# Softmax maxima of an attention kernel: subtracted over whole q tiles, or sent by DMA into a spare row of q

## The chip, the cores and the metric

The kernel is one program on one core of a Trainium2 chip. Its time is the device time of one execution in microseconds (us); several executions give a median. The core has a matrix engine (TensorE, in the profile PE, its weight loads PEld), a vector engine (VectorE, DVE), a scalar engine (ScalarE, ACT), GpSimd (POOL) and a sync engine (SyncE, SP), which here only issues transfers (DMAs).

## What is computed

The input `x` is (16, 512, 128) in float32. Six residual stages follow each other; the first three (a mixture of experts, a linear attention, the experts again) are the front part, which the change leaves alone, and the last three are the back part:

```
x = x + 0.5 * mlp(norm(x))          # front part ends with this one
x = x + attention(norm(x))          # back part, below
x = x + 0.5 * mlp(norm(x))          # back part: w1 (128 x 512), relu, w2

def attention(x):                   # 16 heads of 8 columns, 512 positions
    xn = layernorm(x) * scale + bias
    q, k, v = heads(xn @ wq), heads(xn @ wk), heads(xn @ wv)
    probs = softmax(q @ k.T / sqrt(128))
    return merge(probs @ v) + xn
```

The softmax subtracts the maximum of each row of scores before the exponential, and divides by the row's sum after the product with v.

## The kernel before

The back part (`build_back`) takes one of 16 batches of 512 positions after the other. Heads go in four groups g of four; in a group each head j has a strip of 32 partitions. `qt[g]` and `kt_[g]` hold q and k of a group with the head's 8 numbers as high and low parts in rows 0 to 23 of a strip. Row 24 (`MAX_ROW`) of k's strips is one, and of q's strips zero. These tiles are made by way of memory: `stage` writes the parts (`khi`, `klo`, `qhi`, `qlo`) to a staging buffer, `fetch` reads two 256 KB tiles per group back.

Scores are computed twice. `first_scores` (L1379) makes rows of scores for a block of 128 queries into a bank `MX`, and DVE's `maximum` (L1263) reduces it to the maximum of each query, in tile `nm`. Once the 16 maxima columns of a group are there, PE transposes `nm` (small work "nm": four 128x128 transposes, L1341) and DVE subtracts the result from the q tile into `qm` (L1220). The second scores (L1366, into a bank `ST`) use `qm`: row 24 is then minus the maximum, times k's one. ACT takes the exponential (L1163), and `weighted` (L1394, eight recorded matmuls a step, into `PV`) multiplies by v.

A batch is 16 steps k, written out by hand and the same on every engine. In step k PE issues: `ST` and `MX` matmuls of heads 0 and 1, then `weighted` of step k-1, then those of heads 2 and 3, then the step's small work. The `MX` matmuls and the maxima run `AHEAD` steps before the `ST` matmuls. The table `SMALL` says which small work stands at the end of which step, as (name, batch relative to this one, number):

- xt, kp, qp, v: transposed input, then k, q and v of the next batch. ACT copies the high part of xt, kp, qp; DVE subtracts it (`xl`, `klo`, `qlo`) after the second maximum of the following step.
- nm: the transpose of the maxima. ot: the outputs of a head group transposed, then divided by DVE (L1230, L1232).
- ft, g, y: input, four hidden blocks and two output halves of the MLP of the previous batch; `fl` is ft's low part on DVE.

Results go to seven PSUM banks in two rings. v and g use the three `ST` banks, all other small work the four `MX` banks, in the order in which PE issues them (`ST_RING`, `MX_RING`); `wait_bank` makes a matmul wait until the entry four places (three in `ST`) before it in the ring has been read. DVE also does two layer-norm statistics (`stats`), for the next batch at the start of step 0 and for the MLP input at the start of step 3; GpSimd turns them into `xn`, `xf` and `zf`.

SP issues all transfers in one queue, in program order, and waits in between for the semaphores that free or fill a tile.

Of the kernel before, what the change touches and what calls it, by code (L numbers as in the profile page):

```python
# [106 lines left out]
def build_front(nc, weights, x_dram, mid_dram, ident_dram, turns):  # L107
# [739 lines left out]

AHEAD = 6  # L850
# [30 lines left out]
def build_back(nc, weights, mid_dram, out_dram, staged_dram, tail_dram, batches):  # L881
    w = weights
    with ExitStack() as ctx:
# [16 lines left out]
        khi, klo, qhi, qlo = (sb(n, [P, T, P], F32R) for n in ("khi", "klo", "qhi", "qlo"))  # L900
        qt = [sb(f"qt{g}", [P, T, P], F32R) for g in range(GRP)]
        kt_ = [sb(f"kt{g}", [P, T, P], F32R) for g in range(GRP)]
        qm = [sb(f"qm{k}", [P, T, P], F32R) for k in range(2)]
        nm = [sb(f"nm{k}", [P, T, P]) for k in range(2)]
        va = [sb(f"va{p}", [P, T, H, 32]) for p in range(2)]
        pr = [sb(f"pr{k}", [P, HG, N]) for k in range(2)]
        oTs = [sb(f"oTs{k}", [P, T, P]) for k in range(2)]
# [93 lines left out]
        @block.sync  # L1001
        def _(sp):
            def stage(B, which, tile, part):

                sp.dma_start(staged_dram[B.parity, which][:, part * DH:(part + 1) * DH, :],
                             tile[:].rearrange("p a b -> p (a b)").bitcast(F32)).then_inc(staged.sem, 16)

            def stage_batch(B):
                if not B.exists:
                    return  # L1010
                sp.wait_ge(khi_ready.sem, B.at(khi_ready, 1))
                stage(B, 0, khi, 0)
                free_strips(B, 0)
                stage(B, 0, khi, 1)
                sp.wait_ge(used["kp"].sem, B.at(used["kp"], 1))
                stage(B, 0, klo, 2)
                sp.wait_ge(qhi_ready.sem, B.at(qhi_ready, 1))
                stage(B, 1, qhi, 0)
                stage(B, 1, qhi, 2)
                sp.wait_ge(used["qp"].sem, B.at(used["qp"], 1))  # L1020
                stage(B, 1, qlo, 1)
                if B.first:
                    sp.wait_ge(preset, 64)
                sp.wait_ge(staged.sem, B.at(staged, 16 * 6))

            def free_strips(B, g):

                if not B.first:
                    sp.wait_ge(made["st"].sem, B.at(made["st"], HG * T * (g + 1) - UNITS))

            def fetch(B, g):

                if not B.exists:
                    return
                if g > 0:
                    free_strips(B, g)
                for which, tile in ((0, kt_[g]), (1, qt[g])):
                    sp.dma_start(tile[:].rearrange("p a b -> p (a b)").bitcast(F32),
                                 staged_dram[B.parity, which][g * HG:(g + 1) * HG].rearrange("h r n -> (h r) n")
                                 ).then_inc(fetched[g].sem, 16)  # L1040

            def batch_steps(B):
                nxt, prv, ahead = B + 1, B + -1, B + 2
                if ahead.exists:
                    if B.exists:

                        sp.wait_ge(xx_ready.sem, B.at(xx_ready, 1))
                    p = ahead.parity
                    sp.dma_start(x[p][:], md[ahead.number + PAD]).then_inc(loaded[p].sem, 16)
                fetch(B, 3)  # L1050
                stage_batch(nxt)
                for g in range(3):
                    fetch(nxt, g)
                if prv.exists:
                    p = prv.parity
                    sp.wait_ge(used["y"].sem, prv.at(used["y"], 2))
                    sp.dma_start(od[prv.number], res[p][:]).then_inc(stored[p].sem, 16)

            sp.dma_start(x[0][:], md[PAD]).then_inc(loaded[0].sem, 16)
            for p in range(2):  # L1060
# [124 lines left out]
        def _(dve):  # L1185
# [14 lines left out]
            def small(B, rel, name, n):  # L1200
# [14 lines left out]
                elif name == "ft":  # L1215
                    dve.wait_ge(fh_ready.sem, C.at(fh_ready, 1))
                    nc.vector.tensor_tensor(fl[:], m[:], fh[:], ALU.subtract).then_inc(used["ft"].sem, 1)
                elif name == "nm":
                    dve.wait_ge(made["nm"].sem, C.at(made["nm"], n + 1))
                    nc.vector.tensor_tensor(qm[n % 2][:], qt[n][:], m[:], ALU.subtract).then_inc(used["nm"].sem, 1)  # L1220
                elif name == "ot":
                    dve.wait_ge(made["ot"].sem, C.at(made["ot"], n + 1))
                    if n > 0 or not C.first:
# [30 lines left out]
            def maximum(B, rel, u):  # L1254

                C = B + rel
                if not C.exists:
                    return
                g, t, j = u // (HG * T), u // HG % T, first_head(u)
                dve.wait_ge(made["mx"].sem, C.at(made["mx"], u + 1))  # L1260
                c = 32 * j + MAX_ROW
                bank = MX[MX_PLACE["mx", rel, u] % MX_BANKS]
                nc.vector.tensor_reduce(nm[g % 2][:, t, c:c + 1], bank[:].rearrange("p a b -> p (a b)"), AX.X,  # L1263
                                        ALU.max).then_inc(used["mx"].sem, 1)

            def batch_steps(B):
                for k in range(STEPS):
# [7 lines left out]
                    maximum(B, rel, s * HG + 2)  # L1275
                    maximum(B, rel, s * HG + 3)
                    for name, r, n in SMALL[k]:
                        if name not in FOR_ACT + BY_BOTH:
                            small(B, r, name, n)

            for k in range(2):
# [5 lines left out]
        def _(pe):  # L1287
# [22 lines left out]
            def small(B, rel, name, n):  # L1310
# [26 lines left out]
                                       skip_group_check=True)  # L1337
                elif name == "nm":
                    pe.wait_ge(used["mx"].sem, C.at(used["mx"], (n + 1) * HG * T))
                    for t in range(T):  # L1340
                        mm = pe.transpose(m[:, t], nm[n % 2][:, t], w["ident"][:])  # L1341
                elif name == "ot":
                    pe.wait_ge(pv_out.sem, C.at(pv_out, n + 1))
                    for t in range(T):
# [12 lines left out]
            def scores(B, k, j):  # L1357
# [2 lines left out]
                    return  # L1360
                g, u = k // T, k * HG + j
                if k % T == 0 and j == 0:
                    pe.wait_ge(used["nm"].sem, B.at(used["nm"], g + 1))
                place = ST_PLACE["st", 0, u]
                wait_bank(B, ST_RING, ST_BANKS, place)
                pe.matmul(flat(ST[place % ST_BANKS]), kt_[g][rows_of(j), k % T], flat(qm[g % 2])[rows_of(j)], start=True,  # L1366
                          stop=True).then_inc(made["st"].sem, 1)

            def first_scores(B, rel, u):
# [297 lines left out]
```

## Time and profile before

| | |
|---|---|
| median of 3 executions | 2253.99 us (2253.25 to 2261.86) |
| profiled execution, its own time | 2249.78 us |
| its span, first to last instruction | 2248.0 us |
| PE busy | 1996.7 us (89%) |
| DVE busy | 1687.3 us (75%) |
| ACT busy | 1083.7 us (48%) |
| GpSimd busy | 585.0 us (26%) |
| granted clock of PE, mean | 0.970 |
| transfers | 85.28 MB, mean 38 GB/s |

The back part fills the span from about 1295 us on. A share of the span says little here, as the front part has other limits; the rows are read in the back part alone, and one batch of it in the window 1700 to 1760 us. Busy times of single instructions overlap: two maxima of 0.68 us that follow each other start 0.60 us apart. In a timeline, a row "x4" holds four instructions that ran on without a gap worth telling; its time is from the first's start to the last's end.

### The profile page before, as it was taken

How to read it: one execution, taken by the hardware profiler on the slowest of the kernel's cores; microseconds unless marked ns; L12 is line 12 of the kernel's file. 1: busy time of each engine (PE TensorE's matmuls, PEld its weight loads, DVE VectorE, ACT ScalarE, POOL GpSimd, SP SyncE). 2: the span in 40 equal slices, each digit the busy share in tenths (PEclk: the TensorE clock that was granted, in tenths of full speed). 3: DMA queues.
4: the chain of work that ended last, by engine and by line, in shares of the span. 5: the costliest groups of instructions: out<-in, count | busy, mean ns of one | idle time of the engine just before them, and what ended most of it. 6: DMA issues, size and time to landing. Idle time of an engine off the chain costs nothing. (4 is left out here: it accounts for less than half of the span.)

```text
span 2248.0 us, 34225 instructions
## 1 busy us (share of the span) xinstructions
PE 1996.7 (89%) x12660; PEld 1369.6 (61%) x12660; DVE 1687.3 (75%) x4160; ACT 1083.7 (48%) x1907; POOL 585.0 (26%) x621
## 2 busy tenths in 40 slices
PE   3998989898999899889989758999999999999997
PEld 3787778777877787777877623444444444444443
DVE  5767776767766776767677449888888888888882
ACT  3333323333333333333333117777777777777774
POOL 2331332223222323233313031222222222222211
PEclk9999999999999999999999959999999999999999
DMA  3000000000000000000000032222222222222220
GB/s 117 6 10 10 1 10 10 10 1 10 10 10 5 6 10 10 10 1 10 10 6 1 10 98 71 76 76 76 76 75 76 76 76 76 76 76 79 70 69 10
DMA packets 47941, 85.28 MB, mean 38 GB/s; under 512 B 5728, under 2 KB 9056, under 8 KB 47712
## 3 DMA queue, kind: packets, MB, share of 16 engines
q1 hardware_dynamic: 45872, 81.32, 11.4%
q8 instruction: 101, 1.65, 0.3%
q10 hardware_dynamic: 1904, 1.78, 0.2%
q14 instruction: 64, 0.52, 0.1%
HBM read 49.26 MB, written 34.87 MB: 37 GB/s over the span
## 5 line engine op out<-in xcount | busy, mean ns | idle before, releaser
L1263 DVE TENSOR_REDUCE b_nm<-b_MX 128x1 f32<-128x512 f32 x1024 | 647.6, 682 | 74.1 <-PE b_MX L1379 66.8
L1163 ACT ACTIVATE b_pr<-b_ST 128x512 f32<-128x512 f32 x1024 | 550.8, 601 | 163.1 <-PE b_ST L1366 161.9
L1379 PE MATMUL b_MX<-b_kt,b_qt 32*128 32x512 f32 x1024 | 353.9, 511 | 43.0 <-DMA b_qt<-staging 10.1
L383 ACT ACTIVATE s<-G 128x512 f32<-128x512 f32 x306 | 182.9, 598 | 432.7 <-PE G L685 423.7
L690 PE MATMUL Y<-w_wd,h 128*128 128x128 f32 x2448 | 335.3, 281 | 8.6 <-DVE h L544 7.9
L690 PEld LDWEIGHTS Y<-w_wd,h 128*128 128x128 f32 x2448 | 315.4, 195 | 24.0 <-DVE h L544 13.3
L535 DVE TENSOR_TENSOR su<-U,s 128x512 f32<-128x512 f32 x272 | 186.1, 684 | 161.3 <-ACT s L383 83.3
L1366 PEld LDWEIGHTS b_ST<-b_qm,b_kt 32*128 32x128 f32 x1024 | 119.1, 185 | 304.6 <-ACT b_pr L1163 190.8
L1366 PE MATMUL b_ST<-b_qm,b_kt 32*128 32x512 f32 x1024 | 293.6, 503 | 10.8 <-ACT b_pr L1163 10.7
L1394 PE MATMUL b_PV<-b_pr,b_va 128*32 128x512 f32 x2048 | 280.5, 620 | 0.0
L544 DVE TENSOR_TENSOR h<-C,su 128x512 f32<-128x512 f32 x272 | 188.1, 691 | 9.3
L1379 PEld LDWEIGHTS b_MX<-b_kt,b_qt 32*128 32x128 f32 x1024 | 140.0, 187 | 79.7 <-DVE b_nm L1263 15.5
L683 PE MATMUL U<-xh,w_wuh 128*128 128x512 f32 x306 | 128.2, 419 | 57.5 <-DVE su L535 44.0
L305 POOL TENSOR_TENSOR vpe_s<-mv_s,w_eps 128x4 f32<-128x4 f32 x33 | 6.6, 199 | 627.3 <-DVE mv_s L437 627.3
L1082 POOL TENSOR_TENSOR b_ve<-b_mv,w_eps_two 128x4 f32<-128x4 f32 x16 | 3.2, 201 | 617.5 <-DVE b_mv L1197 617.4
L683 PE MATMUL G<-xh,w_wgh 128*128 128x512 f32 x306 | 145.7, 476 | 0.0
L685 PE MATMUL G<-xl,w_wgh 128*128 128x512 f32 x306 | 121.2, 396 | 0.0
L685 PE MATMUL U<-xl,w_wuh 128*128 128x512 f32 x306 | 121.1, 396 | 0.0
L684 PE MATMUL G<-xh,w_wgl 128*128 128x512 f32 x306 | 121.0, 395 | 0.0
L684 PE MATMUL U<-xh,w_wul 128*128 128x512 f32 x306 | 120.8, 395 | 0.0
L683 PEld LDWEIGHTS U<-xh,w_wuh 128*128 128x128 f32 x306 | 57.7, 189 | 96.9 <-DVE su L535 58.8
L718 PE MATMUL C<-cT,w_pairs 128*128 128x512 f32 x272 | 109.6, 403 | 0.0
(237 smaller groups left out, 3497.3 us busy)
## 6 DMA issues: line engine op xcount, KB each, us to landing
b_kt<-staging SPq DMA_DIRECT2D x64, 256.0 KB, 2.9
b_qt<-staging SPq DMA_DIRECT2D x64, 256.0 KB, 3.4
staging<-b_khi SPq DMA_DIRECT2D x32, 256.0 KB, 3.0
staging<-b_qhi SPq DMA_DIRECT2D x32, 256.0 KB, 3.0
xin<-in_x SPq DMA_DIRECT2D x17, 256.0 KB, 2.6
mid<-xo SPq DMA_DIRECT2D x17, 256.0 KB, 2.0
b_x<-mid SPq DMA_DIRECT2D x16, 256.0 KB, 2.9
staging<-b_klo SPq DMA_DIRECT2D x16, 256.0 KB, 3.0
```

The costliest lines, as they stand in the source:

```text
L383: nc.scalar.activation(sbuf_s[n % 2][:], G[n % 2][:], ACT.Silu).then_inc(act_done.sem, 1)
L535: nc.vector.tensor_tensor(out[:], U[:], sbuf_s[n % 2][:], ALU.mult).then_inc(up_used.sem, 1)
L544: nc.vector.tensor_tensor(h[n % 3][:], C[:], su[n % 2][:], ALU.mult).then_inc(h_ready.sem, 1)
L683: pe.matmul(flat(bank), wh, flat(high), start=True, stop=False)
L684: pe.matmul(flat(bank), wl, flat(high), start=False, stop=False)
L685: return pe.matmul(flat(bank), wh, flat(low), start=False, stop=True)
L690: mm = pe.matmul(bank[:, t], hid[:, t], wd, start=(first and t == 0), stop=True, skip_group_check=True)
L1163: nc.scalar.activation(pr[k % 2][:, j], bank[:].rearrange("p a b -> p (a b)"), ACT.Exp, scale=SM_SCALE).then_inc(used["st"].sem, 1)
L1263: nc.vector.tensor_reduce(nm[g % 2][:, t, c:c + 1], bank[:].rearrange("p a b -> p (a b)"), AX.X, ALU.max).then_inc(used["mx"].sem, 1)
L1366: pe.matmul(flat(ST[place % ST_BANKS]), kt_[g][rows_of(j), k % T], flat(qm[g % 2])[rows_of(j)], start=True, stop=True).then_inc(made["st"] ...
L1379: pe.matmul(flat(MX[place % MX_BANKS]), qt[g][rows_of(j), u // HG % T], flat(kt_[g])[rows_of(j)], start=True, stop=True).then_inc(made["mx ...
L1394: mm = pe.matmul(flat(PV)[rows_of(j)], va[B.parity][:, kt, g * HG + j], pr[k % 2][:, j], start=(kt == 0), stop=(kt == T - 1), skip_group_c ...
```

## The change

The subtraction over q tiles goes, and `qm` with it: the second scores read `qt[g]` itself. The maxima of a group are kept as 16 columns of a 128x32 tile. PE transposes it in one matmul into 32 rows of a bank, ACT copies these with factor -1 into `nr`, and SP sends them in four transfers of 4 rows of 128 numbers (2 KB each) into row 24 of the four strips of `qt[g]` (`shift`). PE waits for these transfers (`shift_in[g]`) before the first `ST` matmul of a group. `AHEAD` is 7 where it was 6, and `SMALL` is rearranged.

```diff
-AHEAD = 6
+AHEAD = 7
 SMALL = [
-    [], [("ot", -1, 3)], [("nm", 0, 1)], [("xt", 1, 0)],
-    [("kp", 1, 0)], [("ot", 0, 0), ("qp", 1, 0)], [("nm", 0, 2)], [("ft", -1, 0)],
-    [("g", -1, 0)], [("ot", 0, 1), ("g", -1, 1)], [("nm", 0, 3)], [("g", -1, 2)],
-    [("g", -1, 3)], [("ot", 0, 2)], [("nm", 1, 0), ("y", -1, 0)], [("v", 1, 0), ("y", -1, 1)]]
+    [], [("nm", 0, 1), ("ot", -1, 3)], [("xt", 1, 0)], [("kp", 1, 0)],
+    [("qp", 1, 0)], [("nm", 0, 2), ("ot", 0, 0)], [("v", 1, 0)], [("ft", -1, 0)],
+    [("g", -1, 0)], [("nm", 0, 3), ("ot", 0, 1)], [("g", -1, 1)], [("g", -1, 2)],
+    [("g", -1, 3)], [("nm", 1, 0), ("ot", 0, 2)], [("y", -1, 0)], [("y", -1, 1)]]
...
-        qm = [sb(f"qm{k}", [P, T, P], F32R) for k in range(2)]
-        nm = [sb(f"nm{k}", [P, T, P]) for k in range(2)]
+        nm = [sb(f"nm{k}", [P, 32]) for k in range(2)]
+        nr = [sb(f"nr{k}", [32, P], F32R) for k in range(2)]
...
+            def shift(C, g):
+                if not C.exists:
+                    return
+                sp.wait_ge(used["nm"].sem, C.at(used["nm"], g + 1))
+                for t in range(T):
+                    sp.dma_start(qt[g][MAX_ROW::32, t].bitcast(F32),
+                                 nr[g % 2][t * HG:(t + 1) * HG].bitcast(F32)).then_inc(shift_in[g].sem, 16)
...
+                elif name == "nm":
+                    if n >= 2 or not C.first:
+                        before = (C, n - 2) if n >= 2 else (C + -1, n + GRP - 2)
+                        act.wait_ge(shift_in[before[1]].sem, before[0].at(shift_in[before[1]], 16 * T))
+                    nc.scalar.activation(nr[n % 2][:], m[0:32, 0], ACT.Copy, scale=-1.0).then_inc(used["nm"].sem, 1)
...
-                elif name == "nm":
-                    nc.vector.tensor_tensor(qm[n % 2][:], qt[n][:], m[:], ALU.subtract).then_inc(used["nm"].sem, 1)
...
-                    for t in range(T):
-                        mm = pe.transpose(m[:, t], nm[n % 2][:, t], w["ident"][:])
+                    mm = pe.transpose(m[0:32, 0], nm[n % 2][:], w["ident"][:])
...
-                    pe.wait_ge(used["nm"].sem, B.at(used["nm"], g + 1))
+                    pe.wait_ge(shift_in[g].sem, B.at(shift_in[g], 16 * T))
```

On PE, between the steps 9 and 10 of a batch, stood the transposes of a group's outputs and the three matmuls of a hidden block, then the matmuls of step 10 (before):

```order
L1345 MATMUL b_MX<-w_ident,b_oTs 128x128 x4
L1292 MATMUL b_ST<-b_fh,w_w1h 128x512
L1293 MATMUL b_ST<-b_fh,w_w1l 128x512
L1294 MATMUL b_ST<-b_fl,w_w1h 128x512
L1366 MATMUL b_ST<-b_qm,b_kt 128x512
L1379 MATMUL b_MX<-b_kt,b_qt 128x512
L1366 MATMUL b_ST<-b_qm,b_kt 128x512
L1379 MATMUL b_MX<-b_kt,b_qt 128x512
L1394 MATMUL b_PV<-b_pr,b_va 32x512 x4
```

In the same place of the changed kernel the one transpose of the maxima and those of the outputs stand, and the hidden block comes a step later:

```order
L1362 MATMUL b_MX<-w_ident,b_nm 32x128
L1366 MATMUL b_MX<-w_ident,b_oTs 128x128 x4
L1387 MATMUL b_ST<-b_qt,b_kt 128x512
L1400 MATMUL b_MX<-b_kt,b_qt 128x512
L1387 MATMUL b_ST<-b_qt,b_kt 128x512
L1400 MATMUL b_MX<-b_kt,b_qt 128x512
L1415 MATMUL b_PV<-b_pr,b_va 32x512 x4
```

Two entries of the `MX` ring now stand between the last `MX` matmul of step 9 and the first of step 10, where one stood; the same holds after the steps 1, 5 and 13.

On PE at the turn from one batch to the next stood, before, the last of v's twelve matmuls and the MLP's second output half:

```order
L1335 MATMUL b_ST<-w_wvl,b_xh 128x128
L1336 MATMUL b_ST<-w_wvh,b_xl 128x128
L1350 MATMUL b_MX<-w_w,b_hid 128x128 x8
L1366 MATMUL b_ST<-b_qm,b_kt 128x512
L1379 MATMUL b_MX<-b_kt,b_qt 128x512
```

In the changed kernel:

```order
L1400 MATMUL b_MX<-b_kt,b_qt 128x512
L1371 MATMUL b_MX<-w_w,b_hid 128x128 x8
L1387 MATMUL b_ST<-b_qt,b_kt 128x512
L1400 MATMUL b_MX<-b_kt,b_qt 128x512
```

The twelve matmuls for v moved to the end of step 6.

On DVE, from the maxima of the steps 0 and 1 to the low part of q (before):

```order
L1263 TENSOR_REDUCE b_nm<-b_MX 128x1 x4
L1220 TENSOR_TENSOR b_qm<-b_qt,b_MX 128x512
L1191 BN_STATS b_stf<-b_xf 128x6 x4
L1195 MEMSET b_nudge 128x1
L1197 BN_AGGR b_mvf<-b_stf 128x2 x4
L1263 TENSOR_REDUCE b_nm<-b_MX 128x1 x6
L1208 TENSOR_TENSOR b_xl<-b_MX,b_xh 128x512
L1263 TENSOR_REDUCE b_nm<-b_MX 128x1 x4
L1211 TENSOR_TENSOR b_klo<-b_MX,b_khi 128x512
```

In the changed kernel:

```order
L1285 TENSOR_REDUCE b_nm<-b_MX 128x1 x4
L1213 BN_STATS b_stf<-b_xf 128x6 x4
L1217 MEMSET b_nudge 128x1
L1219 BN_AGGR b_mvf<-b_stf 128x2 x4
L1285 TENSOR_REDUCE b_nm<-b_MX 128x1 x2
L1230 TENSOR_TENSOR b_xl<-b_MX,b_xh 128x512
L1285 TENSOR_REDUCE b_nm<-b_MX 128x1 x4
L1233 TENSOR_TENSOR b_klo<-b_MX,b_khi 128x512
L1285 TENSOR_REDUCE b_nm<-b_MX 128x1 x4
L1236 TENSOR_TENSOR b_qlo<-b_MX,b_qhi 128x512
```

The subtraction `qm` is gone, and the low parts come one step (four maxima) earlier, while the statistics stay where they were.

## Rows read from the trace of the kernel before

**Rows 1.** The page: busy time of each engine (share of the span), number of instructions.

```profile
PE 1996.7 (89%) x12660; PEld 1369.6 (61%) x12660; DVE 1687.3 (75%) x4160; ACT 1083.7 (48%) x1907; POOL 585.0 (26%) x621
```

**Rows 2.** Chain that ended last, window 1700 to 1760 us, shares by line.

```profile
by line: DVE b_nm L1263 23.8%; PE b_PV L1394 17.7%; PE b_ST L1366 16.9%; PE b_MX L1350 6.1%; PE b_MX L1379 4.9%; PE b_MX L1345 3.9%; PE b_ST L1292 3.6%; PE b_ST L1293 2.3%; PE b_ST L1294 2.3%; DVE b_qm L1220 2.0%; PE b_MX L1341 2.0%; issue 
```

**Rows 3.** Groups by line, 1340 to 2248 us: busy us, mean ns | idle before.

```profile
L1263 DVE TENSOR_REDUCE b_nm<-b_MX 128x1 f32<-128x512 f32 x997 | 631.2, 682 | 63.7 <-PE b_MX L1379 56.4
...
L1220 DVE TENSOR_TENSOR b_qm<-b_qt,b_MX 128x512 fp32r<-128x512 f32 x63 | 42.6, 676 | 1.9 <-PE b_MX L1341 1.9
```

**Rows 4.** Timeline of PE, 1700 to 1760 us: start us, us, what.

```profile
1701.36 1.07 PE L1394 MATMUL b_PV<-b_pr,b_va 128*32 128x512 f32 x8
...
1704.53 1.06 PE L1394 MATMUL b_PV<-b_pr,b_va 128*32 128x512 f32 x8
...
1705.96 0.66 PE L1341 MATMUL b_MX<-w_ident,b_nm 128*128 128x128 f32 x4
...
1707.26 1.06 PE L1394 MATMUL b_PV<-b_pr,b_va 128*32 128x512 f32 x8
...
1713.54 1.07 PE L1394 MATMUL b_PV<-b_pr,b_va 128*32 128x512 f32 x8
...
1716.28 1.06 PE L1394 MATMUL b_PV<-b_pr,b_va 128*32 128x512 f32 x8
...
1720.55 1.07 PE L1394 MATMUL b_PV<-b_pr,b_va 128*32 128x512 f32 x8
...
1721.98 0.33 PE L1334 MATMUL b_ST<-w_wvh,b_xh 128*128 128x128 f32 x1
...
1723.37 2.00 PE L1350 MATMUL b_MX<-w_w,b_hid 128*128 128x128 f32 x16
...
1726.31 1.07 PE L1394 MATMUL b_PV<-b_pr,b_va 128*32 128x512 f32 x8
...
1750.31 1.06 PE L1394 MATMUL b_PV<-b_pr,b_va 128*32 128x512 f32 x8
...
1753.04 1.07 PE L1394 MATMUL b_PV<-b_pr,b_va 128*32 128x512 f32 x8
...
1756.76 1.07 PE L1394 MATMUL b_PV<-b_pr,b_va 128*32 128x512 f32 x8
```

**Rows 5.** Timeline of DVE, the same window.

```profile
1704.66 2.72 DVE L1263 TENSOR_REDUCE b_nm<-b_MX 128x1 f32<-128x512 f32 x4
1707.30 0.68 DVE L1220 TENSOR_TENSOR b_qm<-b_qt,b_MX 128x512 fp32r<-128x512 f32 x1
...
1731.85 0.25 DVE L1230 RECIPROCAL b_rden<-b_MX 128x16 f32<-128x16 f32 x1
...
1732.34 2.47 DVE L1263 TENSOR_REDUCE b_nm<-b_MX 128x1 f32<-128x512 f32 x4
...
1740.08 0.68 DVE L1208 TENSOR_TENSOR b_xl<-b_MX,b_xh 128x512 fp32r<-128x512 f32 x1
...
1743.91 0.68 DVE L1211 TENSOR_TENSOR b_klo<-b_MX,b_khi 128x512 fp32r<-128x512 f32 x1
...
1748.12 0.68 DVE L1214 TENSOR_TENSOR b_qlo<-b_MX,b_qhi 128x512 fp32r<-128x512 f32 x1
...
1754.27 0.68 DVE L1217 TENSOR_TENSOR b_fl<-b_MX,b_fh 128x512 fp32r<-128x512 f32 x1
```

**Rows 6.** Timeline of GpSimd, the same window: the last operation of `xn`.

```profile
1732.35 1.28 POOL L1098 TENSOR_TENSOR b_xn<-b_xn,w_lnsb 128x512 f32<-128x512 f32 x1
```

**Rows 7.** Timeline of SP's queue: one transfer issued behind another.

```profile
1752.46 0.43 SPq L1038 DMA_DIRECT2D b_qt<-staging  x1
```

**Rows 8.** Transfers by line: count, KB each, median us from issue to landing.

```profile
b_qt<-staging SPq DMA_DIRECT2D x64, 256.0 KB, 3.4
...
w_bq<-in_bq SPq DMA_DIRECT2D x1, 0.5 KB, 6.4
```

**Rows 9.** Groups of ACT, whole span: the smallest reads of a PSUM bank.

```profile
L362 ACT ACTIVATE lb<-Z 128x64 f32<-128x64 f32 x34 | 7.6, 223 | 66.5 <-PE Z L677 66.5
```

More of the change, by code:

```diff
@@ L856 @@
 SMALL = [
[4 rows of a table removed]
[4 rows of a table added]
 FOR_ACT = ("v", "g")
 BY_BOTH = ("xt", "kp", "qp", "ft")
+IN_ACT = FOR_ACT + BY_BOTH + ("nm",)
 def ahead_of(k):
@@ L939, in build_back @@
         fetched = [sig(f"fetched{g}", 32) for g in range(GRP)]
+        shift_in = [sig(f"shift_in{g}", 16 * T) for g in range(GRP)]
         preset = ctx.enter_context(nc.semaphore("b_preset"))
@@ L1023, in stage_batch @@
                     sp.wait_ge(preset, 64)
-                sp.wait_ge(staged.sem, B.at(staged, 16 * 6))
             def free_strips(B, g):
@@ L1050, in batch_steps @@
                 fetch(B, 3)
+                shift(B, 1)
                 stage_batch(nxt)
-                for g in range(3):
-                    fetch(nxt, g)
+                shift(B, 2)
+                if nxt.exists:
+                    sp.wait_ge(staged.sem, nxt.at(staged, 16 * 6))
+                fetch(nxt, 0)
+                fetch(nxt, 1)
+                shift(B, 3)
+                fetch(nxt, 2)
+                shift(nxt, 0)
                 if prv.exists:
@@ L1130, in small @@
                 C = B + rel
-                if not C.exists or name not in FOR_ACT + BY_BOTH:
+                if not C.exists or name not in IN_ACT:
                     return
@@ L1217, in small @@
                     nc.vector.tensor_tensor(fl[:], m[:], fh[:], ALU.subtract).then_inc(used["ft"].sem, 1)
-                elif name == "nm":
-                    dve.wait_ge(made["nm"].sem, C.at(made["nm"], n + 1))
-                    nc.vector.tensor_tensor(qm[n % 2][:], qt[n][:], m[:], ALU.subtract).then_inc(used["nm"].sem, 1)
                 elif name == "ot":
@@ L1260, in maximum @@
                 dve.wait_ge(made["mx"].sem, C.at(made["mx"], u + 1))
-                c = 32 * j + MAX_ROW
+                if u % (HG * T) == 0 and (g >= 2 or not C.first):
+                    before = (C, g - 1) if g >= 2 else (C + -1, g + GRP - 1)
+                    dve.wait_ge(made["nm"].sem, before[0].at(made["nm"], before[1]))
+                c = t * HG + j
                 bank = MX[MX_PLACE["mx", rel, u] % MX_BANKS]
-                nc.vector.tensor_reduce(nm[g % 2][:, t, c:c + 1], bank[:].rearrange("p a b -> p (a b)"), AX.X,
+                nc.vector.tensor_reduce(nm[g % 2][:, c:c + 1], bank[:].rearrange("p a b -> p (a b)"), AX.X,
                                         ALU.max).then_inc(used["mx"].sem, 1)
@@ L1277, in batch_steps @@
                     for name, r, n in SMALL[k]:
-                        if name not in FOR_ACT + BY_BOTH:
+                        if name not in IN_ACT:
                             small(B, r, name, n)
@@ L1362, in scores @@
                 if k % T == 0 and j == 0:
-                    pe.wait_ge(used["nm"].sem, B.at(used["nm"], g + 1))
+                    pe.wait_ge(shift_in[g].sem, B.at(shift_in[g], 16 * T))
                 place = ST_PLACE["st", 0, u]
                 wait_bank(B, ST_RING, ST_BANKS, place)
-                pe.matmul(flat(ST[place % ST_BANKS]), kt_[g][rows_of(j), k % T], flat(qm[g % 2])[rows_of(j)], start=True,
+                pe.matmul(flat(ST[place % ST_BANKS]), kt_[g][rows_of(j), k % T], flat(qt[g])[rows_of(j)], start=True,
                           stop=True).then_inc(made["st"].sem, 1)
```

## The prediction

> **What bounds the kernel now.** I began with the busy times of the page. They leave no engine clearly ahead: PE 89% and DVE 75% of a span of which the back part, where the change is, is only the last two fifths [rows 1]. In the back part alone DVE is busy with maxima for most of the time, and still waits 56.4 us in all for the matmuls that feed them [rows 3]. So I read the chain of waits over one batch: it changes engines, about a quarter in the maxima and most of the rest in PE's matmuls, and the two things that the change attacks, the subtraction `qm` and the transposes of the maxima, hold 2.0% each of 60 us, 1.2 us each [rows 2]. A share of a chain is not a saving, because what comes late after it may be late anyway. Therefore I used the timelines of PE and DVE and cut a batch by the starts of the eight matmuls on `PV`, one set per step.
>
> Step 9 starts its set at 1701.36, step 0 of the next batch at 1726.31, step 9 again at 1756.76 [rows 4]. A batch is 24.95 + 30.45 = 55.4 us. The two parts have different limits. From step 9 to step 0 PE paces: a step with four transposes or none takes 2.73 (1704.53 to 1707.26), the two with a hidden block 6.28 together, the one with the maxima's transposes and the first output half 4.27, the one with v and the second half 5.76 [rows 4]. From step 0 to step 9 DVE paces, with maxima 0.60 apart and the low parts between them [rows 5].
>
> **Second half of a batch, steps 9 to 0.** The removed `qm` is worth nothing here, since DVE waits for PE. What counts is PE's own list. The transposes of the maxima leave the output step: 0.59 of 4.27 (1705.96 to the following matmul, just under the row's 0.66), 3.68 stays. v leaves the last step: its matmuls start 1.39 ahead of the output half [rows 4]; I take 1.45, so 4.31 stays of 5.76. That is 2.04 saved. Three hidden blocks in three steps cost 3 x 3.14 = 9.42, as two cost 6.28.
>
> The price stands in steps 9 and 13. Two entries of the `MX` ring follow each other there, so the second `MX` matmul of the next step reuses the bank of the fourth maximum of this step; with one entry it was the third's. In step 10 the maxima start 0.13 after the `PV` set (1704.66 against 1704.53) and the fourth is done at 2.77 (`qm` starts at 1707.30) [rows 4, 5]. Only then may that matmul start, and `PV` 0.43 later: 2.8 + 0.43 = 3.25 for such a step instead of 2.73. New sum: 3.25 + 9.42 + 3.25 + 3.68 + 4.31 = 23.91, against 24.95: 1.04 us less.
>
> **First half, steps 0 to 9.** I walk DVE from the start of step 2's maxima, 1732.34 [rows 5]. After step 1 there are two entries again. The last maximum of step 1 ends about 1731.9 (the reciprocal starts at 1731.85), so `PV` of step 2 starts at 1732.4, the third `MX` matmul 1.0 later and its maximum 0.5 after that, at 1733.87: DVE does two maxima, waits 0.3, does two, and reaches the statistics at 1735.08. From 1734.74 (four maxima) to `xl` at 1740.08 it now takes 5.34 for `qm`, statistics and six maxima [rows 5]. Without `qm` (0.59) and four maxima (2.40) 2.35 stays, so `xl` starts at 1737.43. Each low part holds a bank that the fourth `MX` matmul of its step needs, with a product behind it: `xl` to `klo` is 3.83 (1740.08 to 1743.91), and `klo` to `qlo` becomes the same: `qlo` at 1745.1. It was 1748.12, one step later.
>
> From `qlo` to the next `PV` set was 2.19 (1748.12 to 1750.31) with four transposes; with five, and the wait on the fourth maximum, I take 2.4: step 6 at 1747.5. Then comes v, in a step that PE paces: 4.27 - 0.59 - 1.85 (an output half, a bit under the row's 2.00) + 1.45 = 3.3, where the plain step is 2.73. Step 8 starts at 1747.5 + 3.3 + 2.73 = 1753.5, and with `fl` and a hidden block 3.72 (1753.04 to 1756.76), plus 0.1 since its maxima can't start before their step, step 9 at 1757.35 [rows 4]. That is 31.04 from step 0 against 30.45: 0.59 us more. The early projections and the missing `qm` are eaten by v and by DVE's waits.
>
> **Work that lies beside.** The copy with factor -1 on ACT: not shown before. Between 0.22 (64 columns by 128 partitions) [rows 9] and 0.60 for a whole bank; for 128 columns I take 0.28, near the lower end. It comes after the fourth exponential, and the next one can't start before about 0.5 later, since the longer small work holds up its scores: hidden at 0.28, 0.1 out in the open at 0.60. GpSimd's `xn` is ready at 1733.63 [rows 6]; PE now wants it at 1732.4 + 1.43 = 1733.85. Hidden, with only 0.2 to spare.
>
> The four transfers: SP issues one per 0.43 [rows 7]. Tightest is group 3: copy done 3.3 after the `PV` set of step 9, last issue at 4.75, and PE wants the row at 3.25 + 6.28 - 0.43 = 9.1. So 4.3 us may pass until landing. Nothing so small between on-chip tiles is in the trace: the bounds are 3.4 for a fetch of 256 KB and 6.4 for 0.5 KB in a crowd of loads at the start [rows 8]. I take 3.4 or less, as the fetches stand in the same queue and the same part; hidden. The fetches that now queue behind a shift have a step or more to spare.
>
> SP goes on after 0.43 us, without waiting for the 3.4 us to landing [rows 7, 8], so transfers of one queue are under way together. The Trainium skill (DMA: Bandwidth & Descriptors, Rules for kernel authors) advises to merge small transfers, under 64 KB being mostly overhead, and its section Anatomy of one DMA has some 2 us fixed per transfer. Taken as four in a row that estimate would be 8 us, over the slack; overlapped, 2 us, and nothing. No row here shows a small one alone.
>
> **Sum.** Per full batch -1.04 + 0.59 = -0.45; 14 such batches: -6.3. The first batch has no MLP work to gain from and pays the two waits (+1.0); ahead of it v no longer stands before the first scores, against a seventh step of maxima (-0.7); the last batch -0.5. Together -6.5. The profiled execution took 2249.78 and would take 2243.3; the median is 4.2 above it, so I forecast **2247.5 us**. A measurement tells 0.5%, 11.3 us, from no change; this is less. By itself the forecast has 2238 to 2257, 0.7 us per batch to either side.
>
> **Rivals.**
> - *The work removed is all gained* (0.28). The 2.4 us of chain per batch [rows 2], less 0.4 for the remaining transpose, times 15 is 30 us: 2224. For it: the chain runs through both. Against it: the bank waits above. Without these waits alone (0.52 + 0.52 + 0.3) I would come to 2229.
> - *The shifted rows come late* (0.07), slower. If landing takes over 4.3 us, PE stands still at the first scores of a group. With 6.4 [rows 8] group 3 is 2.1 late, group 2 about 1.8, the others 0.5 together: 4.4 x 16 = 70 us, 2318. Against it: 3.4 for much more data. Should the four even land one after the other, 3.4 each, the last lands at 3.3 + 13.6 = 16.9, 7.8 late: 125 us for group 3 alone, 2372 or more (0.01 of the 0.07). [...]
> - *ACT's copy is in the way* (0.13), slower. ACT works in order; where it isn't hidden, 0.28 to 0.60 four times a batch is 18 to 38 us: 2265 to 2285, and PE idles before the scores on the exponentials. It decides once the copy waits for a transpose that DVE delays.
> - *v and the wait for `xn`* (0.06): if `xn` is 0.5 late, and the chain of k and q with it, 7 us are added: 2255.
>
> The forecast itself has 0.46. Faster by over 0.5%: all of the first rival and a sixth of the forecast, 0.36. Slower: the two middle rivals but for a part of the second of them, 0.17. The same: 0.47. The range of 8 in 10 is 2222 to 2268.
>
> **What would show it.** Right: `qm` gone from the chain; `PV` sets 3.2 to 3.3 apart after steps 1, 9 and 13, with PE waiting on the maxima there; last step of a batch 4.3; 55.0 us per batch; ACT's copy under 0.3; no wait of PE on a transfer to `qt`. Wrong: `PV` sets 2.8 apart after 9 and 13 (then the first rival), a PE wait on `qt` from `nr`, or step 6 far from 3.3.

## The result, and the profile after

| | median us (runs) | lowest to highest | profiled execution: us, span, clock |
|---|---|---|---|
| before | 2253.62 (6) | 2248.83 to 2264.79 | 2249.78, 2248.0, 0.970 |
| after | 2276.46 (6) | 2262.22 to 2282.18 | 2262.22, 2260.4, 0.964 |

After over before is 1.0084 [1.0056, 1.0112]: slower, by 23 us between the medians. The forecast was 2247.5 us, range 2222 to 2268: a little faster, and the kernel is slower, above the range. In a later comparison (10 runs of after, 25 of before) the ratio was 1.0059 [1.004, 1.0078], 17 us between the medians: the direction stands, and the size is known to some 6 us.

The six times of after line up with the mean granted clock of each run: 2262.2 and 2264.7 us at 0.964, 2275.7 at 0.957, 2277.2 to 2278.9 at 0.953 to 0.954, 2282.2 at 0.951. That was the first lead.

The page of after, answering to [rows 1], and below it the two groups of lines that answer to [rows 3], here over the whole span. Columns: busy us, mean ns | idle before, what ended most of it.

```profile
PE 2002.6 (89%) x12468; PEld 1356.4 (60%) x12468; DVE 1658.4 (73%) x4096; ACT 1089.2 (48%) x1971; POOL 584.8 (26%) x621
...
L1285 DVE TENSOR_REDUCE b_nm<-b_MX 128x1 f32<-128x512 f32 x1024 | 655.4, 683 | 123.6 <-PE b_MX L1400 114.7
...
L1400 PE MATMUL b_MX<-b_kt,b_qt 32*128 32x512 f32 x1024 | 363.2, 516 | 62.0 <-DVE b_xl L1230 23.0
```

DVE lost 64 instructions and 29 us of work, PE lost 192 matmuls, and yet PE is busy 6 us longer. The copy and the transfers behave as forecast: the copy of the maxima's row on ACT takes 256 ns, and SP issues four transfers in 2.27 us (the first row: groups of ACT from 1340 us on; the second: timeline of SP: start, us).

```profile
L1169 ACT ACTIVATE b_nr<-b_MX 32x128 fp32r<-32x128 f32 x63 | 16.1, 256 | 2.5 <-PE b_MX L1362 2.5
```

```profile
1756.38 2.27 SPq L1049 DMA_DIRECT2D b_qt<-b_nr  x4
```

Cut by the starts of the `PV` sets as in the prediction, a batch reads (us per step, steps 0 to 15; one batch of each kernel without a disturbance):

| | 0 | 1 | 2 | 3 | 4 | 5 | 6 | 7 | 8 | 9 | 10 | 11 | 12 | 13 | 14 | 15 | sum |
|---|---|---|---|---|---|---|---|---|---|---|---|---|---|---|---|---|---|
| before | 2.76 | 2.74 | 2.87 | 4.16 | 3.72 | 4.22 | 3.52 | 2.73 | 3.72 | 3.15 | 2.73 | 3.09 | 3.19 | 2.74 | 4.27 | 5.76 | 55.4 |
| after | 2.76 | 3.33 | 2.73 | 4.90 | 3.82 | 3.77 | 3.36 | 2.73 | 3.72 | 3.33 | 3.09 | 3.09 | 3.19 | 3.33 | 3.85 | 4.42 | 55.4 |

Undisturbed, the two kernels are equal. But 9 of the 14 full batches of after are longer than that, by 0.5 to 2.0 us, 10.9 us in all, in steps 3 to 5; step 3 goes up to 6.15, step 4 to 5.09, step 5 to 4.24. I call these disturbed. In before it is 5 of 14, 5.5 us in all, in steps 4 and 5, step 4 up to 5.00. In before they are batches 2, 5, 8, 11 and 14, every third one, so they are not scattered by chance. One of the long batches of after, timeline of PE (start, us, what, then in brackets idle before and what ended it):

```profile
1743.83 0.50 PE L1387 MATMUL b_ST<-b_qt,b_kt 32*128 32x512 f32 x1
1745.97 0.50 PE L1400 MATMUL b_MX<-b_kt,b_qt 32*128 32x512 f32 x1 [1.64 <-DVE b_xl L1230]
1746.40 0.50 PE L1314 MATMUL b_MX<-b_xh,w_wkh 128*128 128x512 f32 x1
...
1747.87 1.94 PE L1415 MATMUL b_PV<-b_pr,b_va 128*32 128x512 f32 x8
...
1750.65 0.79 PE L1314 MATMUL b_MX<-b_xh,w_wq1h 128*128 128x512 f32 x1
...
1752.96 1.72 PE L1415 MATMUL b_PV<-b_pr,b_va 128*32 128x512 f32 x8
...
1754.61 0.49 PE L1400 MATMUL b_MX<-b_kt,b_qt 32*128 32x512 f32 x1
```

The same `PV` set that takes 1.07 elsewhere takes 1.94 here, and a matmul of 0.50 takes 0.79. The windows of one microsecond name the reason (columns: length; busy us of PE, PEld, DVE, ACT, POOL with counts; PEclk; DMA share; GB/s):

```profile
1743.00:1744.00 1.00, 1.00 (x11) 0.17 (x3) 0.96 (x8) 1.00 (x3) 0.97 (x1) 1.00 0.00 0
1744.00:1745.00 1.00, 0.33 (x3) 0.01 (x3) 1.00 (x5) 0.82 (x3) 0.69 (x2) 1.00 0.00 0
1745.00:1746.00 1.00, 0.03 (x1) 0.03 (x1) 1.00 (x3) 0.45 (x1) 0.92 (x2) 1.00 0.00 0
...
1747.00:1748.00 1.00, 1.00 (x10) 0.33 (x12) 0.20 (x2) 0.60 (x2) 1.00 (x2) 0.75 0.00 0
1748.00:1749.00 1.00, 1.00 (x8) 0.06 (x6) 1.00 (x2) 1.00 (x2) 1.00 (x1) 0.50 0.00 0
...
1753.00:1754.00 1.00, 1.00 (x12) 0.16 (x8) 0.91 (x2) 0.94 (x2) 0.00 (x0) 0.50 0.00 0
1754.00:1755.00 1.00, 1.00 (x11) 0.19 (x3) 0.98 (x2) 0.14 (x1) 0.00 (x0) 0.83 0.79 182
```

PE is almost idle from 1744.3 to 1746.0, and from about 1747.5 to 1754.3 the granted clock is 0.50, that is 1.2 instead of 2.4 GHz. How did so long a wait come about? From the list of PE's waits in the back part of after (us in all, times, longest):

```profile
PE b_MX L1400 <- DVE b_xl L1230: 23.0, 14, 1.6
```

and of before:

```profile
PE b_MX L1326 <- DVE b_nm L1263: 14.6, 14, 1.0
...
PE b_MX L1379 <- DVE b_xl L1208: 4.7, 10, 0.5
```

Before, PE stood still 1.0 us ahead of the transposes of `xn` and 0.5 us for `xl`, with 3.1 us of matmuls between (timeline of PE in the same batch, before):

```profile
1737.23 0.66 PE L1326 MATMUL b_MX<-w_ident,b_xn 128*128 128x128 f32 x4 [1.04 <-DVE b_nm L1263]
...
1740.82 0.49 PE L1379 MATMUL b_MX<-b_kt,b_qt 32*128 32x512 f32 x1 [0.47 <-DVE b_xl L1208]
```

After, the transposes stand one step earlier, in step 2, ahead of the statistics of `xf` that DVE works off at the start of step 3. Maxima, statistics and `xl` then follow each other on DVE with nothing that PE could do between them, and its two waits are one, of 1.64 us. The timeline of DVE in the long batch above shows the row of work at whose end PE goes on (`xl` ends at 1745.92, the matmul starts at 1745.97):

```profile
1742.87 0.86 DVE L1213 BATCH_NORM_STATS2 b_stf<-b_xf 128x6 f32<-128x128 f32 x4
...
1744.07 1.26 DVE L1285 TENSOR_REDUCE b_nm<-b_MX 128x1 f32<-128x512 f32 x2
1745.24 0.68 DVE L1230 TENSOR_TENSOR b_xl<-b_MX,b_xh 128x512 fp32r<-128x512 f32 x1
```

The 12.4 us between the profiled executions divide so: up to the first `PV` set +1.3 (1340.85 to 1342.19), batch 0 +3.9, batches 1 to 14 +5.9 (of it 5.4 disturbances), batch 15 -0.1, the tail +1.3. The first of these differs as much between two executions of one kernel: in a second profile of after the first `PV` set starts at 1343.64. Batch 0 ran at a mean granted clock of 0.83 where it had 0.91 before, and the tail at 0.72 instead of 0.80; in the second profile of after batch 0 had 0.92 and was 0.8 us longer than before, so most of the 3.9 is the clock again. The tail was 26.4 us in both profiles of after, against 25.1.

### The profile page after: what moved, and what is told of

Same layout as the page of the kernel before. It is cut to its first block and busy times, and to the rows that moved or that the text cites. A ratio compares the mean times of both kernels' runs of the same rounds, so it can differ in the third digit from the quotient of the medians.

```text
span 2260.4 us, 34221 instructions
## 1 busy us (share of the span) xinstructions
PE 2002.6 (89%) x12468; PEld 1356.4 (60%) x12468; DVE 1658.4 (73%) x4096; ACT 1089.2 (48%) x1971; POOL 584.8 (26%) x621
## 5 line engine op out<-in xcount | busy, mean ns | idle before, releaser
L1285 DVE TENSOR_REDUCE b_nm<-b_MX 128x1 f32<-128x512 f32 x1024 | 655.4, 683 | 123.6 <-PE b_MX L1400 114.7
L1400 PE MATMUL b_MX<-b_kt,b_qt 32*128 32x512 f32 x1024 | 363.2, 516 | 62.0 <-DVE b_xl L1230 23.0
L1387 PE MATMUL b_ST<-b_qt,b_kt 32*128 32x512 f32 x1024 | 303.1, 507 | 11.1 <-ACT b_pr L1185 9.5
L1387 PEld LDWEIGHTS b_ST<-b_qt,b_kt 32*128 32x128 f32 x1024 | 122.6, 186 | 310.9 <-ACT b_pr L1185 201.4
L1415 PE MATMUL b_PV<-b_pr,b_va 128*32 128x512 f32 x2048 | 285.8, 632 | 0.0
L683 PE MATMUL U<-xh,w_wuh 128*128 128x512 f32 x306 | 127.9, 418 | 57.2 <-DVE su L535 44.1
```

The source lines that it names most:

```text
L683: pe.matmul(flat(bank), wh, flat(high), start=True, stop=False)
L1285: nc.vector.tensor_reduce(nm[g % 2][:, c:c + 1], bank[:].rearrange("p a b -> p (a b)"), AX.X, ALU.max).then_inc(used["mx"].sem, 1)
L1400: pe.matmul(flat(MX[place % MX_BANKS]), qt[g][rows_of(j), u // HG % T], flat(kt_[g])[rows_of(j)], start=True, stop=True).then_inc(made["mx ...
L1415: mm = pe.matmul(flat(PV)[rows_of(j)], va[B.parity][:, kt, g * HG + j], pr[k % 2][:, j], start=(kt == 0), stop=(kt == T - 1), skip_group_c ...
```

## The experiments

**Theory.** The path through the row costs nothing in a batch that runs undisturbed. The new order puts PE's waits together into one of 1.6 us, and around the end of this wait the clock falls in most batches. **Rivals:** the copy and the transfers cost the time; or the small slowings of single steps add up and the clock merely shows it.

### The order alone, and the path alone

The maxima by subtraction on DVE as before, with the order of after (7 steps ahead):

```
-AHEAD = 6
+AHEAD = 7
...
-    [], [("ot", -1, 3)], [("nm", 0, 1)], [("xt", 1, 0)],
-    [("kp", 1, 0)], [("ot", 0, 0), ("qp", 1, 0)], [("nm", 0, 2)], [("ft", -1, 0)],
-    [("g", -1, 0)], [("ot", 0, 1), ("g", -1, 1)], [("nm", 0, 3)], [("g", -1, 2)],
-    [("g", -1, 3)], [("ot", 0, 2)], [("nm", 1, 0), ("y", -1, 0)], [("v", 1, 0), ("y", -1, 1)]]
+    [], [("nm", 0, 1), ("ot", -1, 3)], [("xt", 1, 0)], [("kp", 1, 0)],
+    [("qp", 1, 0)], [("nm", 0, 2), ("ot", 0, 0)], [("v", 1, 0)], [("ft", -1, 0)],
+    [("g", -1, 0)], [("nm", 0, 3), ("ot", 0, 1)], [("g", -1, 1)], [("g", -1, 2)],
+    [("g", -1, 3)], [("nm", 1, 0), ("ot", 0, 2)], [("y", -1, 0)], [("y", -1, 1)]]
```

> The new step table and 7 steps ahead, with the old subtraction on DVE. Clock theory (the slower time of the changed kernel comes from one long wait of PE, 1.6 us on xl in step 3, after which the granted clock falls to 1.2 GHz for some microseconds in most batches): the wait stands here too and is longer by the subtraction after step 1 (0.6 us on DVE ahead of it), so step 3 is near 5 us or more, most batches lose 0.5 to 2 us to the clock, 2265 to 2290 us. Rival (the transfers, or ACT's copy, cost the time): without them it comes out at or below the kernel before, 2240 to 2255.

The row path with the order of before; the list of small work goes the other way round:

```
-AHEAD = 7
+AHEAD = 6
...
```

> The old step table and 6 steps ahead, with the new path of the maxima (one transpose, copy on ACT, four transfers). Clock theory: step 3 has two short waits as before, so as few disturbed batches as before (5 of 14); but only one full step lies between the maxima and the scores, so PE waits for the transfers in groups 1 to 3 if they land later than 2 us after the last issue: an undisturbed batch of 54 to 57 us, and the size of the waits measures the landing. Rival (the path itself is what costs): a batch over 56 us with waits that the changed kernel shows too.

| | median us (runs) | to before [95%] | undisturbed batch | disturbed of 14 |
|---|---|---|---|---|
| order alone | 2280.85 (4) | 1.0116 [1.0093, 1.0139] | 55.7 | 11 |
| path alone | 2276.48 (4) | 1.0106 [1.0076, 1.0136] | 56.4 | 1 |

Each half alone is slower than before, for different reasons. The order alone has the 1.6 us wait and the disturbed batches, up to 2.8 us longer each. (The expectation had the wait longer by the subtraction; it is the same, and step 3 takes 4.90.) PE's waits with the order alone:

```profile
PE b_MX L1379 <- DVE b_xl L1208: 23.6, 15, 1.6
```

The path alone has nearly no disturbed batch, 1 where 5 were expected, and without the subtraction its steps 3 and 6 are 0.4 us shorter each. But step 7 takes 3.75 instead of 2.73 and step 11 3.72 instead of 3.09, a batch 1.0 us more. Its first waits of PE in the back part are for the shifted row, which after does not wait for once (the 2.4 stands in the last batch, the longest in a full batch is 1.24, in step 7):

```profile
PE b_ST L1387 <- DMA b_qt<-b_nr: 42.8, 47, 2.4
PE b_ST L1387 <- ACT b_pr L1185: 9.7, 20, 1.1
PE b_MX L1348 <- DVE b_nm L1285: 8.9, 14, 0.7
```

The wait of 1.24 us stands in step 7 of all 14 full batches, and the clock falls behind one of them only (batch 11, steps 8 and 9 at 4.99 each). So a wait that stands alone and is shorter by 0.4 us did it once in 14, with batches of another length.

This run gives the price of landing, which before did not show. SP issues the four from 1745.65 on, and the score that needs the last of them starts at 1748.91 (timelines of SP and of PE with the path alone):

```profile
1745.65 2.15 SPq L1049 DMA_DIRECT2D b_qt<-b_nr  x4
```

```profile
1748.91 0.49 PE L1387 MATMUL b_ST<-b_qt,b_kt 32*128 32x512 f32 x1 [0.35 <-DMA b_qt<-b_nr]
```

The fourth is issued about 1747.3, half a microsecond ahead of the end of the row, so it was there at the latest 1.6 us after its issue (an estimate from these two rows). With 7 steps ahead this is hidden, with 6 not. So the new order hides the transfers that the path needs, and brings the wait with it.

### The same kernel with the wait filled

Six repetitions of one score matmul, in step 3, where PE waits for `xl`. They overwrite a score with itself and take 1.65 us; nothing else is changed.

```
+for extra in range(6 if (k, j) == (3, 3) else 0):
+    pe.matmul(flat(ST[place % ST_BANKS]), kt_[g][rows_of(j), k % T], flat(qt[g])[rows_of(j)],
+              start=True, stop=True)
```

> The changed kernel, in which PE issues the fourth score matmul of step 3 seven times instead of once (same operands, same bank), so that it has work for about 1.3 of the 1.6 us for which it waits for xl. Clock theory: the clock stays up, no more than 5 of 14 batches are disturbed, the undisturbed batch stays at 55.4 us, and the time falls by 8 to 15 us against the changed kernel, to 2250 to 2262. Rival (the clock falls for another reason, or its fall is not what costs): the same count of disturbed batches and 2265 to 2285 us.

Measured: 2260.51 us (10 runs), 1.0029 [1.0011, 1.0046] to before; 5 disturbed batches of 14 instead of 9. The undisturbed batch stays at 55.44: the extra work is free where PE stood. Timeline of PE in such a batch:

```profile
1804.70 1.65 PE L1388 MATMUL b_ST<-b_qt,b_kt 32*128 32x512 f32 x6
1806.19 0.39 PE L1390 MATMUL b_ST<-b_qt,b_kt 32*128 32x512 f32 x1
1806.84 0.50 PE L1403 MATMUL b_MX<-b_kt,b_qt 32*128 32x512 f32 x1 [0.25 <-DVE b_xl L1230]
```

Copy, transfers and undisturbed steps are those of after, so neither rival can make this difference. The count is still that of before, and not none. To have the comparison on one chip the changed kernel ran again, beside a version with more filling (8 repetitions in step 3, 3 each in steps 4 and 5):

> The changed kernel once more, beside the others on one chip. Clock theory: 2262 to 2282 us, and the executions line up by their mean granted clock (0.964 to 0.951), since only the count of disturbed batches differs; undisturbed batches stay at 55.4 us. Rival: the spread has another source and the clock is the same in slow and fast executions.

> As the filled kernel, with eight repeated score matmuls in step 3 and three each in steps 4 and 5, where PE waits 0.6 us for klo and qlo. Clock theory: fewer disturbed batches than with six (6 of 14), 2245 to 2260 us, the undisturbed batch at 55.4 to 55.7. Rival (repeating matmuls merely shifts other work): no fewer disturbed batches, and a longer undisturbed one.

After again: 2269.35 us (10), 1.0059 [1.004, 1.0078], 8 disturbed batches. More filling: 2261.3 (10), 1.0037 [1.0016, 1.0059], 4 disturbed batches of +1.15 each. More work for PE, and 8 us less between the medians; the two intervals overlap, so this pair alone would be a hint. It missed the 2245 to 2260 expected by a little (and the expectation counts 6 disturbed batches of the filled kernel, where it has 5): the filling of steps 4 and 5 brings nothing measurable, and the remaining drops come without a long wait in step 3.

### The statistics of xf moved away

`if k == 3 and prv.exists` decides where the statistics stand. In step 6 DVE has time for them:

```
-                if k == 3 and prv.exists:
+                if k == 6 and prv.exists:
```

> The changed kernel with the MLP's layer-norm statistics (1.2 us of DVE) at the start of step 6, where v's matmuls let DVE wait, instead of step 3. Clock theory: the wait for xl falls from 1.6 to about 0.4 us, few batches are disturbed, step 3 takes 3.7 to 3.9 us instead of 4.9 and step 6 stays near 3.4 to 3.6: 54.3 to 54.7 us per batch, 2225 to 2245 us in all. Rival (GpSimd's zf comes too late for step 7): PE waits there up to 1 us, and the batch stays over 55 us.

Measured: 2239.1 us (4), 0.9934 [0.9908, 0.996]. No batch of 14 is disturbed, and each takes 54.3: step 3 went from 4.90 to 3.72, which makes 16 us over 14 batches. That is a gain of its own, apart from the clock. Between this profile (2232.07) and the second one of after (2262.98) lie 30.9 us: 29.4 in the batches 1 to 14, of which 16 are the shorter step and 13 the disturbances that are gone. The mean clock is 0.970 to 0.976 here. The wait on `xl`, 0.6 us where 0.4 was expected, is one of many of the same length:

```profile
PE b_MX L1400 <- DVE b_klo L1233: 8.6, 15, 0.6
PE b_MX L1400 <- DVE b_qlo L1236: 8.6, 15, 0.6
PE b_MX L1400 <- DVE b_fl L1239: 7.6, 15, 0.6
PE b_MX L1400 <- DVE b_xl L1230: 7.1, 15, 0.6
```

### The inverse: a long wait put into the kernel before

The kernel before, with its own order and its subtraction, and the statistics one step later, so that its two waits become one:

```
-                if k == 3 and prv.exists:
+                if k == 4 and prv.exists:
```

> The kernel before, with only the MLP's layer-norm statistics moved from the start of step 3 to the start of step 4, where the low part xl stands, so that PE's two short waits (1.04 us before the transposes xt, 0.47 us on xl) become one of about 1.6 us on xl, as in the changed kernel. DVE's work and its order of maxima per batch are the same. Clock theory: the undisturbed batch stays at 55.4 us within 0.2, but 8 or more of 14 batches are disturbed (5 before), 2258 to 2280 us. Rival (the clock falls by itself, whatever PE waits for): 3 to 6 disturbed batches and 2249 to 2258 us.

Measured: 2266.82 us (10), 1.0043 [1.002, 1.0065], with a clock of 0.952 to 0.960 against 0.960 to 0.970 of before beside it. All 14 batches of the profiled execution are disturbed, 56.3 to 57.2 us. It was the slowest of the ten (2276.07, clock 0.952), so others may have fewer. Timeline of PE, and windows of the same place:

```profile
1754.78 0.51 PE L1379 MATMUL b_MX<-b_kt,b_qt 32*128 32x512 f32 x1 [1.65 <-DVE b_xl L1208]
1755.22 0.80 PE L1292 MATMUL b_MX<-b_xh,w_wkh 128*128 128x512 f32 x1
...
1757.53 1.55 PE L1394 MATMUL b_PV<-b_pr,b_va 128*32 128x512 f32 x8
```

```profile
1752.00:1754.00 2.00, 1.14 (x11) 0.19 (x3) 1.96 (x10) 1.96 (x5) 0.89 (x2) 1.00 0.00 0
1754.00:1756.00 2.00, 1.22 (x3) 0.87 (x4) 2.00 (x4) 0.35 (x1) 1.84 (x3) 0.79 0.00 0
1756.00:1758.00 2.00, 2.00 (x11) 0.64 (x13) 0.36 (x2) 0.97 (x2) 1.81 (x2) 0.50 0.00 0
```

So the effect does not need the change: one wait of 1.65 us in the old kernel brings it too. I had expected the undisturbed batch at 55.4 ± 0.2. There was none to measure; the shortest is 56.33. But every step is undisturbed in some batch (step 3 at 2.99, step 4 at 4.89 and step 5 at 4.22), and these lengths add up to 55.4. So the move costs nothing but what comes with the clock.

### The ring wait, and a faster kernel

The prediction charged 0.52 us each to steps 9 and 13, in which two entries of the `MX` ring follow each other. To test that by itself, the two output transposes go one step later:

```
-    [("g", -1, 0)], [("nm", 0, 3), ("ot", 0, 1)], [("g", -1, 1)], [("g", -1, 2)],
-    [("g", -1, 3)], [("nm", 1, 0), ("ot", 0, 2)], [("y", -1, 0)], [("y", -1, 1)]]
+    [("g", -1, 0)], [("nm", 0, 3)], [("ot", 0, 1), ("g", -1, 1)], [("g", -1, 2)],
+    [("g", -1, 3)], [("nm", 1, 0)], [("ot", 0, 2), ("y", -1, 0)], [("y", -1, 1)]]
```

> The changed kernel with the outputs' transposes moved from steps 9 and 13 to steps 10 and 14, so that no two entries of the MX ring follow each other there. If the wait on the fourth maximum is the price of these steps, 9 and 13 fall from 3.33 to 2.74 us, step 10 stays near 3.15, step 14 grows by 0.4 to 0.6: an undisturbed batch of 54.7 to 54.9 us. The wait for xl stays, so the clock theory still wants most batches disturbed: 2250 to 2272 us. Rival (these steps are long for ACT's copy or the transfers): they stay at 3.3.

Measured: an undisturbed batch of 54.70, steps 9 and 13 at 2.73 instead of 3.33, steps 10 and 14 at 3.16 and 4.25 instead of 3.09 and 3.85. Before and after the move, step 9 in the timeline of PE; first the kernel after:

```profile
1709.69 1.06 PE L1415 MATMUL b_PV<-b_pr,b_va 128*32 128x512 f32 x8
...
1712.60 0.49 PE L1400 MATMUL b_MX<-b_kt,b_qt 32*128 32x512 f32 x1
1713.02 1.07 PE L1415 MATMUL b_PV<-b_pr,b_va 128*32 128x512 f32 x8
```

its DVE:

```profile
1709.82 2.73 DVE L1285 TENSOR_REDUCE b_nm<-b_MX 128x1 f32<-128x512 f32 x4 [0.66 <-PE b_MX L1400]
```

and the split:

```profile
2096.90 1.06 PE L1415 MATMUL b_PV<-b_pr,b_va 128*32 128x512 f32 x8
...
2099.63 1.06 PE L1415 MATMUL b_PV<-b_pr,b_va 128*32 128x512 f32 x8
```

In after the fourth maximum ends at 1709.82 + 2.73 = 1712.55, the matmul into its bank starts at 1712.60 and `PV` 0.42 later. The list of waits doesn't show this one, because the modelled ends of the matmuls ahead cover it; the start times do. The whole time of the split came to 2258.73 (10), 1.0025 [0.9996, 1.0054], since 12 of its batches are disturbed: it still has the 1.6 us wait.

Both edits together, and then the remaining two-entry step 1 split too (`ot(-1,3)` in step 0):

> Both edits, the statistics in step 6 and the outputs' transposes apart from the maxima. If both reasons hold they add up: 53.5 to 53.8 us per batch, hardly a disturbed one, 2218 to 2232 us. Rival (once DVE's wait is gone something else limits these steps, as the exponentials do at 2.73): 54.0 or more.

> The kernel with the statistics in step 6 and the outputs' transposes in 10 and 14, and now also those of the last group from step 1 to step 0, so that step 1 has one entry of the MX ring. Ring theory: step 1 falls from 3.33 to 2.74 us, step 0 grows by 0 to 0.4 for PE's wait on ACT's copy of the outputs: 53.0 to 53.4 us per batch, 2220 to 2232 us. Rival (DVE paces there anyway, so the maxima come no earlier): 53.5 us per batch, step 2 longer by what step 1 gains.

| | median us (runs) | to before [95%] | batch | disturbed |
|---|---|---|---|---|
| both | 2235.74 (5) | 0.9911 [0.9886, 0.9936] | 53.57 | 0 |
| and step 1 | 2235.03 (4) | 0.989 [0.9847, 0.9933] | 53.29 | 1 (batch 1) |

Each ratio is to before on the same chip (2252.48 us for the first row, 2259.34 for the second). Both beat before and after. The batches are as expected, 53.5 to 53.8 and 53.0 to 53.4, but both medians lie 3 to 4 us above the times expected. The executions lie in two groups: one of each kernel at 2222.5 and 2223.8, the other seven at 2234 to 2238. The profile of the last kernel is of the second group: in it batch 0 takes 59.2 us instead of some 51.4, at the low clock, and the first `PV` set comes 3.8 us later than in the profile at 2223.83 (windows, columns as above):

```profile
1370.00:1380.00 10.00, 9.01 (x59) 3.61 (x57) 7.36 (x12) 7.10 (x14) 0.00 (x0) 0.83 0.34 105
1380.00:1390.00 10.00, 9.23 (x43) 3.10 (x39) 6.32 (x12) 5.20 (x11) 0.00 (x0) 0.50 0.00 1
1390.00:1400.00 10.00, 9.32 (x41) 3.09 (x45) 6.05 (x10) 5.83 (x13) 0.00 (x0) 0.50 0.18 54
```

## Why the prediction was wrong

**Second half, 23.91 forecast: 24.30.** The mechanism was right in each part: two-entry steps 3.33 (3.25 forecast), three hidden blocks 9.37 (9.42), the output steps 3.85 (3.68) and 4.42 (4.31). Four terms are 0.08 to 0.17 too small, 0.44 us together, as much as the whole gain forecast per batch.

**First half, 31.04 forecast: 31.12.** The walk along DVE held: `xl` 11.24 after step 0 (11.12 forecast), the step with v 3.36 (3.3).

**Net per batch, -0.45 forecast: +0.04.** So the gain of 6.3 us in 14 batches was not there even without the clock. Savings and costs are where the prediction put them, but they came out equal.

**Work beside.** Right: the copy took 0.256 (0.28 forecast), landing 1.6 (3.4 or less), no wait of PE on `qt` from `nr`, `xn` in time. Issue took 0.50 to 0.57 each instead of 0.43, still hidden. Three of the rivals are refuted by this: the shifted rows are not late at 7 ahead (at 6 they are), ACT's copy is not in the way, and `xn` is ready (PE waits for it in no full batch). The first rival, all removed work gained, is refuted by the step lengths.

**First batch, +1.0 forecast.** The one of the second profile of after took 51.80 against 50.97: +0.8. The one of the first had 54.9, with steps 3, 9 and 10 0.5 to 1.5 longer than in the second. The 0.7 ahead of it can't be read: the first `PV` set came between 1340.2 and 1348.6 us in the twelve profiles, all with the same front part. **Last batch, -0.5 forecast: -0.1.**

**The step that failed** is the walk of the first half, and it failed in what it did not ask. It set up where DVE would be and let PE wait for it, "DVE does two maxima, waits 0.3, does two, and reaches the statistics at 1735.08", and counted a wait of PE as free as long as DVE paced the step. It never summed PE's waits into one stretch, and took every matmul at the duration of a row at full clock. With the transposes of `xn` in step 2, the stretch became 1.64 us, and around its end the clock fell in 9 of 14 batches (before: 5). Shown from both sides: with the wait filled there are 5 and 4 disturbed batches, with the wait at 0.6 none, and in the old kernel with one such wait 14 of 14. Each count is of one profiled execution, that of after the fastest of six; the medians go the same way (8 us down with more filling, 7.5 us up in the old kernel). None of the rivals named it either, although before already shows it, in 5 batches whose step 4 takes up to 5.00 instead of 3.72: the prediction cut one batch, and that was one without a disturbance.

**Sizes.** In the profiled execution the disturbances explain 5.4 of the 12.4 us. Undisturbed batches add 0.6, batch 0 adds 3.9, mostly clock again. Against the forecast for this execution, 2243.3, it is 18.9 us more: 6.9 from the batch term (-6.3 forecast, +0.6 measured), 5.4 from the disturbances, 5.0 from batch 0 and what is ahead of it (+0.3 forecast, +5.3 measured), 0.4 from the last batch, 1.3 from the tail. So the clock is the larger part of the miss in this execution, and the mis-sized terms of the batch the second. The median of after lies further from before, since the executions at 0.951 to 0.957 are 13 to 20 us longer than the profiled one; their place in the program is not seen, as only one execution was profiled.

**Open.** Why the drop comes in some batches and not in others with the same wait. The order in which they come (every third one in before, every second one from batch 5 on in the second profile of after) says that the place of the wait in time counts too. Kernels whose batches differ in length, as the path alone and the one with the statistics in step 6, are therefore not a clean comparison of counts; before, after and the filled kernels, all at 55.4, are. Why the filled kernel keeps 5 disturbed batches, and the one with four waits of 0.5 to 0.6 us per batch has none, is open too. Why batch 0 of some executions runs at the low clock; its waits are no longer than in others. What the 7 us are that the filled kernel is still above before, with the same batch and as many disturbances; its profile has the first set 4.9 us later and a batch 0 of 57.2, so most of the excess in it lies ahead of batch 1. A part of that is the filling itself: batch 0 has no long wait in step 3, and its step 3 takes 7.46 us with the repetitions, at the low clock; without them it took 4.49 in the first profile of after (mostly at the low clock) and 3.84 in the second (at the full one).

## What to carry to other kernels

When work is moved, look not only at the sum of PE's waits but at the longest stretch without matmuls: two waits of 1.0 and 0.5 us with work between are not the same as one of 1.6. A wait that costs nothing by itself can be paid for afterwards: here a `PV` set in the next 3 to 7 us took up to 1.94 us instead of 1.07. Cut all repetitions of a stage by their starts, and compare lengths, before taking one of them as the pattern.

## What was not expected of the hardware

- A single wait of PE of 1.64 us, between stretches in which it is fully busy, goes with a fall of the granted clock from 2.4 to 1.2 GHz in 9 of 14 batches of after and 14 of 14 of the old kernel with such a wait. The fall starts between 0.5 us ahead of the end of the wait and 2.1 us after it, and the clock returns 3 to 7 us later. A wait of 1.24 us by itself (the path alone) had it in 1 of 14. The Trainium skill (TensorE: Matmul & The Clock Gate, Why this matters for your kernels) advises to avoid idle gaps of PE between bursts of matmuls. These runs agree with the advice, and the gaps that already matter here are shorter than those it speaks of.
- Useless repetitions of a matmul, in a place where PE would stand still, did not lengthen the batch (55.44 us), and the median was 8 us lower on one chip.
- The last of four transfers of 2 KB between on-chip tiles is there 1.6 us after its issue, and 3.3 us after the issue of the first (1745.65 to 1748.91), so they don't follow one another whole. The Trainium skill (DMA: Bandwidth & Descriptors, Anatomy of one DMA) has some 2 us fixed for a transfer issued by GpSimd; SP issues here, which the prediction left out, and 1.6 is a little below that.
